# Two adapter layers on one core: when the parts of the combined weight C' are made, and which queue fetches the second weight blocks

## The reference, cut to what matters

```python
def layer0(x, ids, W0, b0, A0, B0):      # x: 8 batches x 512 tokens x 2048
    h = einsum('bsd,brd->bsr', x, A0[ids])          # rank 16
    return einsum('bsd,od->bso', x, W0) + b0 + einsum('bsr,bor->bso', h, B0[ids])

def layer1(x, ids, W1, b1, A1, B1):
    h = einsum('bti,bir->btr', x, A1[ids])
    return einsum('bti,oi->bto', x, W1) + b1 + 2.0 * einsum('btr,bro->bto', h, B1[ids])

x = x + layer0(x, itok_B_6_15, ...)
x = x + layer1(x, itok_B_0_23, ...)
```

## Time and profile before

| | |
|---|---|
| median of three executions | 2171.0 us (2167.95 to 2177.97) |
| profiled execution | 2161.93 us, span 2160.2 us, 27571 instructions |
| mean granted TensorE clock | 0.987 of full speed |
| TensorE matmul (PE) | busy 2076.9 us (96%) |
| TensorE weight load (PEld) | 1712.8 us (79%) |
| VectorE (DVE) | 1535.8 us (71%) |
| ScalarE (ACT) | 738.1 us (34%) |
| GpSimd (POOL) | 689.3 us (32%) |
| DMA | 458.03 MB, mean 212 GB/s; SyncE's queue 69.9% of 16 engines' span |

### The profile page before, as it was taken

One profiled execution on the slowest core, in us unless ns is written; L12 is line 12 of the kernel. 1 busy time (PEld: TensorE's weight loads), 2 busy tenths in 40 slices (PEclk: granted clock), 3 DMA queues, 4 the chain that ended last, 5 costly groups with the idle time before them and its releaser, 6 DMA issues.

```text
span 2160.2 us, 27571 instructions
## 1 busy us (share of the span) xinstructions
PE 2076.9 (96%) x9292; PEld 1712.8 (79%) x9292; DVE 1535.8 (71%) x2161; ACT 738.1 (34%) x1294; POOL 689.3 (32%) x498
## 2 busy tenths in 40 slices
PE   6599899999989999999999999999999999999999
PEld 5488687887878788888887888877888788888887
DVE  3367778867778876676876666875767876766875
ACT  5453232323323332333333333332333333333332
POOL 0023121544030445140544130544221445221353
PEclk9799999999999999999999999999999999999999
DMA  9974746798664699474799574789574689574676
GB/s 294 279 239 128 234 145 196 213 277 262 176 185 140 201 266 304 143 222 131 213 259 311 146 224 119 225 246 293 168 217 122 213 242 321 168 215 123 209 218 198
DMA packets 316681, 458.03 MB, mean 212 GB/s; under 512 B 27516, under 2 KB 125820, under 8 KB 316028
## 3 DMA queue, kind: packets, MB, share of 16 engines
q1 hardware_dynamic: 316284, 455.21, 69.9%
q10 hardware_dynamic: 256, 1.05, 0.3%
HBM read 381.70 MB, written 74.45 MB: 211 GB/s over the span
## 4 chain that ended last, share of the span: by engine, by line
PE 73%; DVE 9%; DMA 9%; issue 3%; SPq 2%; ACT 2%; POOL 1%; ACTq 0%; DVEq 0%; POOLq 0%
PE acc L1497 22%; PE acc L1499 21%; PE acc L1498 21%; DMA w_second<-wc_t 4%; DVE w_lo L1031 3%; DMA w_second<-v_t 2%; PE h_acc L1410 2%; PE h_acc L1414 2%; DVE c_out L1193 2%; DVE x_sum L1046 1%; DMA pb_t<-b1d_rows 1%; POOL w_raw L804 1%; DVE c_acc L1132 1%; DVE xop_lo L1056 1%; PE acc L1424 1%
## 5 line engine op out<-in xcount | busy, mean ns | idle before, releaser
L1497 PE MATMUL acc<-xop_hi,w_hi 128*128 128x512 f32 x2688 | 1055.6, 393 | 24.2 <-DVE w_lo L1031 19.1
L804 POOL TENSOR_TENSOR w_raw<-w_raw,w_second 128x512 f32<-128x512 f32 x464 | 652.3, 1407 | 1280.5 <-DMA w_second<-wc_t 862.9
L1498 PE MATMUL acc<-xop_hi,w_lo 128*128 128x512 f32 x2688 | 1048.9, 390 | 0.0
L1499 PE MATMUL acc<-xop_lo,w_hi 128*128 128x512 f32 x2688 | 1048.7, 390 | 0.0
L1031 DVE TENSOR_TENSOR w_lo<-w_raw,w_hi 128x512 fp32r<-128x512 f32 x672 | 568.3, 848 | 446.8 <-ACT w_hi L869 443.7
L869 ACT ACTIVATE w_hi<-w_raw 128x512 fp32r<-128x512 f32 x672 | 423.7, 631 | 1194.7 <-PE acc L1499 980.8
L1497 PEld LDWEIGHTS acc<-xop_hi,w_hi 128*128 128x128 f32 x2688 | 506.2, 188 | 142.1 <-DVE w_lo L1031 31.1
L1499 PEld LDWEIGHTS acc<-xop_lo,w_hi 128*128 128x128 f32 x2688 | 506.1, 188 | 106.4
L1498 PEld LDWEIGHTS acc<-xop_hi,w_lo 128*128 128x128 f32 x2688 | 506.4, 188 | 103.0
L1193 DVE TENSOR_TENSOR c_out<-acc,c_out 128x512 f32<-128x512 f32 x304 | 202.1, 682 | 7.9 <-PE acc L1424 6.2
L1046 DVE TENSOR_TENSOR x_sum<-x_in 128x512 f32<-128x512 f32 x240 | 207.5, 876 | 0.1
(11 more groups left out here) (117 smaller groups left out, 826.7 us busy)
## 6 DMA issues: line engine op xcount, KB each, us to landing
w_raw<-wc_t SPq DMA_DIRECT2D x448, 256.0 KB, 3.8
w_second<-wc_t SPq DMA_DIRECT2D x320, 256.0 KB, 5.0
w_raw<-v_t SPq DMA_DIRECT2D x208, 256.0 KB, 3.8
w_second<-v_t SPq DMA_DIRECT2D x144, 256.0 KB, 5.0
x_in<-x_t SPq DMA_DIRECT2D x128, 256.0 KB, 6.0
out_t<-c_out SPq DMA_DIRECT2D x128, 256.0 KB, 5.4
x_in<-w_t SPq DMA_DIRECT2D x64, 256.0 KB, 5.8
wc_t<-c_out SPq DMA_DIRECT2D x64, 256.0 KB, 5.5
```

The lines of the kernel that those rows point to most:

```text
L804: nc.gpsimd.tensor_tensor(w_raw[:, r, :], w_raw[:, r, :], w_second[:, n % RAW2, :], ALU.add if sign > 0 else ALU.subtract).then_inc(w_summ ...
L1497: nc.tensor.matmul(bank[:, :], wh, xh, start=(k == 0), stop=False)
L1498: nc.tensor.matmul(bank[:, :], wl, xh, start=False, stop=False)
L1499: mm = nc.tensor.matmul(bank[:, :], wh, xl, start=False, stop=end)
```

## The change

Three things are moved; no arithmetic is added or left out.

1. In passes 0 and 1 the `down` of M2 stands behind steps 5 and 7 (before 1 and 3), and the split of the following adapter in M2 in slot 12 (before 8). The four `p_add` stand 4, 9, 14 and 19 slots behind the start of M3 and M4 (before 4, 8, 12, 16), with their loads and stores.
2. The second half of `scale_c` is in M7 (before in M4). The first `turn_c` stays behind step 1 of M7, the second goes behind step 5 of M6 (before step 5 of M7), with `c_reduce` in slot 6 of M6. SyncE waits for the sums accordingly.
3. The `w_second` DMAs of all passes are issued by ScalarE's queue, in its slot g behind w_hi of step g+2, for step g+5 (before by SyncE in slot g for step g+6, behind `w_raw`). The waits are the same.

```diff
+DOWN_AT, A_SPLIT_AT = (1, 3), 8
+DOWN_LATE, A_SPLIT_LATE = (5, 7), 12
...
+        def is_late(pl, i):
+            return pl < PRE and i == M2
...
-            if j == 8 and i in DOWN and pl * 4 + DOWN_ORDER.index(i) + 1 < NPL * 4:
+            if i in DOWN and j == (A_SPLIT_LATE if is_late(pl, i) else A_SPLIT_AT) and pl * 4 + DOWN_ORDER.index(i) + 1 < NPL * 4:
...
-        P_ADD_AT = (4, 8, 12, 16)
+        P_ADD_AT = (4, 9, 14, 19)
...
+        C_TURN_AT = ((M7, 2), (M6, 6))
...
-                (oh, dh), *second = PRODUCTS[i][1]
+                oh, dh = PRODUCTS[i][1][0]
                 col = (dh * KH + h * KS) * P
                 sp.dma_start(w_raw[:, r, :], w_t[oh * MH + m, :, col:col + SW]).then_inc(wa_loaded[r], 16)
-                for oh, dh in second:
-                    n = second_no(s)
-                    if n >= RAW2:
-                        sp.wait_ge(w_summed, STEPS + n - RAW2 + 1)
-                    else:
-                        sp.wait_ge(g_turned, GROUPS)
-                    col = (dh * KH + h * KS) * P
-                    sp.dma_start(w_second[:, n % RAW2, :], w_t[oh * MH + m, :, col:col + SW]
-                                 ).then_inc(wb_loaded[n % RAW2], 16)
...
                     if pl < PRE:
-                        sp.wait_ge(c_scaled, (pl + 1) * 2 * KT)
+                        sp.wait_ge(c_scaled, (pl * 2 + (1 if i == M7 else 2)) * KT)
...
+            def load_second(s):
+
+                if not (STEPS <= s < NG and is_sum_w(s)):
+                    return
...
+                if n >= RAW2:
+                    act_e.wait_ge(w_summed, STEPS + n - RAW2 + 1)
+                else:
+                    act_e.wait_ge(g_turned, GROUPS)
+                col = (dh * KH + h * KS) * P
+                act_e.dma_start(w_second[:, n % RAW2, :], w_source(pl)[oh * MH + m, :, col:col + SW]
+                                ).then_inc(wb_loaded[n % RAW2], 16)
...
                 if g + 2 < NG:
                     w_split_hi(g + 2)
+                load_second(g + 2 + RAW2)
...
-                if pl < PRE and i in (M3, M4):
+                if pl < PRE and i in (M3, M7):
                     scale_c(pl * 2 * KT + (0 if i == M3 else KT) + j)
-                if pl < PRE and i == M7 and j in (2, 6):
-                    c_reduce(pl * 2 + (j == 6))
+                if pl < PRE and (i, j) in C_TURN_AT:
+                    c_reduce(pl * 2 + C_TURN_AT.index((i, j)))
...
-                pe.wait_ge(c_scaled, (pl * 2 + 2) * KT)
+                pe.wait_ge(c_scaled, (n + 1) * KT)
...
-                    if i in DOWN and j in (1, 3):
-                        down(q, range(0, KS) if j == 1 else range(KS, KH))
-                    if pl < PRE and i == M7 and j in (1, 5):
-                        turn_c(pl * 2 + (j == 5))
+                    down_at = DOWN_LATE if is_late(pl, i) else DOWN_AT
+                    if i in DOWN and j in down_at:
+                        down(q, range(0, KS) if j == down_at[0] else range(KS, KH))
+                    if pl < PRE and (i, j + 1) in C_TURN_AT:
+                        turn_c(pl * 2 + C_TURN_AT.index((i, j + 1)))
```

More of the change, by code:

```diff
@@ L920, in h_split_hi @@
                                      bias=h_bias[:, b:b + 1]).then_inc(h_hi_ready, 1)
+            def load_second(s):
+                if not (STEPS <= s < NG and is_sum_w(s)):
+                    return
+                q, j = divmod(s, STEPS)
+                pl, i = divmod(q, NPROD)
+                m, h = ORDER[j]
+                oh, dh = PRODUCTS[i][1][1]
+                n = second_no(s)
+                if s == M2 * STEPS:
+                    for i_v in range(2):
+                        act_e.wait_ge(v_stored[i_v], NU * 16 // 2)
+                    for i_v in range(PRAW):
+                        act_e.wait_ge(part_stored[i_v], NPART // PRAW * 16)
+                if pl == PRE and j == 0 and i in (M5, M2):
+                    for b in range(4):
+                        act_e.wait_ge(out_stored[b], (PRE if i == M2 else 1) * MH * 16)
+                if n >= RAW2:
[5 more added lines that the diff above has]
+                                ).then_inc(wb_loaded[n % RAW2], 16)
             act_e.wait_ge(ids_loaded, 32)
```

## The result

| | before | after |
|---|---|---|
| median of 13 runs (lowest to highest), us | 2168.3 (2162.5 to 2178.0) | 2156.2 (2147.9 to 2163.6) |
| ratio, 95% interval | | 0.9945 (0.9928 to 0.9962) |
| the profiled execution, us (span) | 2161.9 (2160.2) | 2159.9 (2158.2) |

The change makes the kernel faster by 12 us; 20 were forecast. Over thirteen runs the kernel before has its median at 2168.3 us, and not at the 2171.0 of the first three from which the forecast started.

A forecast was written before the change was run, and what follows sets the result against it. TensorE, busy 96%, was taken as the bound, held up by pauses in M2 and M1 of passes 0 and 1. Terms -16.5 - 8.8 + 5.4 + 0 = -19.9 us, from 2171 to 2151 us, range 2136 to 2168.

The forecast's parts named there:

- Part 1: M2 of passes 0 and 1, and a pause in M3: 19.5 us at stake, gain 16.5, ends 12 and 19.5.
- the sign: M2 and M1 of passes 0 and 1: the granted clock would be 1.00 in these stretches.
- round trip of a quarter: Store and load of a p_add quarter: 10.5 us, given 13.6 us by five slots, so VectorE's idle 5.29 and 3.81 us go.
- (d): p_add still waits or VectorE's queue stays long; half of parts 1 and 2 lost, 12.6 us: 2164 us, chance 0.09.
- What is late next: VectorE's own crowd in slots 14 and 15 of M3, falling behind by some 3 us over three slots.
- Part 2: scale_c moved from M4 to M7: gain 8.8 us at M1, loss 5.4 us in M7 over passes 0 and 1.
- price of a scale_c: One scale_c in M7 beside GpSimd's additions: 1.05 us taken, between 0.66 and 1.7, so 16.8 us for sixteen.
- the cover: VectorE in M7: 9.5 us idle plus 3.8 us of lead, 13.3 in all, absorb most of sixteen scale_c's 16.8 us.
- (a): VectorE full in M7, every scale_c meeting a GpSimd addition: 13.9 us lost in each pass, 2173 us, chance 0.10.
- Part 3: w_second issued by ScalarE in all passes: gain taken as 0, ends -8 and +15 us.
- (c): w_second's cycle was the only limit, so 9 us of M6 and M5 go: 2142 us, chance 0.19.
- (b): Transfers left on SyncE's queue come late, w_raw taking 11 us to land: 35 us lost, 2186 us, chance 0.07.

The follow-up runs named there:

- later comparison: The changed kernel, all three parts, timed once more against the kernel before: 2152.9 us against 2168.9, ratio 0.9926 (0.9903 to 0.9949).
- p1_only: Kernel before with only the later down of M2 and the quarters five slots apart: 2153.0 us against 2166.1, ratio 0.9943.
- p2_only: Kernel before with only the second half of scale_c in M7 and the second turn in M6: 2169.2 us against 2166.1, ratio 1.0014.
- scale_spread: Changed kernel with the sixteen scale_c in slots 5 to 10 of M7 and 4 to 13 of M6, second turn behind step 15: 2150.7 us.
- p3_only: Kernel before with only the w_second loads issued by ScalarE's queue: 2158.6 us against 2166.1, ratio 0.9971.
- m7_small_add: Changed kernel with GpSimd's additions for M7 of passes 0 and 1 cut to 8 of 512 columns: 2147.2 us, ratio to before 0.9894.

## Why the prediction was right, and where it wasn't

The forecast was 2151 us in a range of 2136 to 2168, and 2156.2 came out. The sum was -20 and the result -12 (-16 in the later comparison), but its three terms are off by 3 to 8 us, with both signs.

**Part 1: right in mechanism, too high** (-13.1 for -16.5 by the times; the interval reaches from 8 to 17 us). The products give less than that: M3 and M2 of both passes, where the whole term was to come from, lose 8.0 us in p1_only and 9.3 and 9.9 in the two profiles of the change. In pass 1 the change did nearly what was forecast: M2 at 51.7 and 51.1 us for 49 to 51 (51.1 to 53.9 over the nine profiles with part 1, the 53.9 in p1_only), no idle time before `down`. In pass 0 it didn't: M2 stayed at 57.4 us, with a granted clock of 0.94 where 1.00 was named as the sign. The step that failed is the round trip of a quarter, 10.5 us in 13.6. I had added up the DMAs and two issues; but in the same rows the store begins at 235.64, and the second p_add had run 3.5 us earlier. That p_add, in the kernel before and in the changed one:

```profile
232.12 0.42 DVE L1111 TENSOR_TENSOR q_half<-h_acc,q_half 128x256 f32<-128x256 f32 x1
...
235.04 0.42 DVE L1138 TENSOR_TENSOR q_half<-h_acc,q_half 128x256 f32<-128x256 f32 x1
```

The 3.1 us from its end to the issue of the store were left out; with them the time from p_add to p_add was 13.2 us already, with next to nothing to spare, and in the changed kernel it became 17.3, as the store is issued 5.2 us late there and takes 6.9 instead of 5.5 us. The rival that p_add would still wait for its quarter (d) is thus true for pass 0, and in the changed kernel for all the fourth quarters. "What is late next" was answered with VectorE's crowd; first of all it was the next quarter, and the crowd behind it.

**Part 2: gain right, cost too low.** M1's gain is 7.5 us in p2_only (97.8 to 90.3 for both passes), 6.9 and 6.0 in the two profiles of the change; 8.8 were forecast. The cost: M7 and M6 together grow by 4.9 and 4.7 us in p2_only, 9.5 us where 5.4 were forecast, by 6.8 and 18.4 in the two of the change. The price of a scale_c was right: 1.05 us taken, means of 1150 and 964 ns measured in M7 (1029 and 1017 in the second profile). What failed is the cover: "into it go 9.5 us idle and 3.8 us of lead". The lead can be spent once. The crowds at the start of M7 and of M6 spend it already, and the sixteen operations were set through all slots of M7, both boundaries included. So M7 uses up the idle time, and M6 begins with nothing in hand: its steps 1 and 2 take 5.4 and 4.1 us in pass 0, 6.2 and 4.5 in pass 1, for 2.72. scale_spread shows it from the other side: the same work at the same price between the crowds costs these two products nothing. Rival (a), VectorE full in M7, came true in what it names (48.76 busy of 49.02) at a third of its price by p2_only (9.5 of 27.8 us; two thirds and a quarter in the two profiles of the change), for not every scale_c had to meet an addition for M7 to be full.

**Part 3: the sum's zero was wrong, rival (c) right.** p3_only gives 7.5 us where (c) had 9. ScalarE's issues, changed kernel:

```profile
L945 ACTq DMA_DIRECT2D w_second<-wc_t x320: 326/326/362, 828.1 to 2137.9; - x160
...
DMA to landing us min/median/max: 2.9/4.3/7.7
```

An issue takes 0.326 us instead of the 0.43 of the earlier trace rows, and a landing 4.3 us (at most 7.7) instead of 5.0 (9.6). In the stretch where it is tight, from slot 4 of M6 to slot 1 of M5, the median of w_second went from 7.1 us before to 5.9 in p3_only and that of w_raw from 7.1 to 7.8. That is the sharing of which (b) and (c) are the two directions, and both are there: w_raw pays 0.7 us, not the 2.6 of rival (b), which has it land in 11 us for 8.5. The clean M6 of pass 3 agrees with the chain of the earlier trace rows, where one w_second took 8.7 us. That the cycle of the three w_second buffers was the limit is in the trace of the kernel before; GpSimd and the issues of w_second, late in M6 of pass 3:

```profile
1482.75 1.29 POOL L804 TENSOR_TENSOR w_raw<-w_raw,w_second 128x512 f32<-128x512 f32 x1 [2.27 <-DMA w_second<-wc_t]
...
1484.07 0.32 SPq L552 DMA_DIRECT2D w_second<-wc_t  x1
...
1487.26 1.29 POOL L804 TENSOR_TENSOR w_raw<-w_raw,w_second 128x512 f32<-128x512 f32 x1 [3.22 <-DMA w_second<-wc_t]
...
1488.57 0.32 SPq L552 DMA_DIRECT2D w_second<-wc_t  x1
```

Each load is issued 0.03 us after the addition that frees its buffer has ended, and each addition has waited for a w_second. Over the four such stretches before, 53 loads, the median from the buffer free to the issue is 0.03 us, and from the landing to the addition 0.13 us: for most of them neither SyncE's order nor its time for issuing was in the way, only the landing. In p3_only the second of these is 0.46 us, and additions wait for w_raw too. A fourth buffer wasn't tried, as there is no room for it.
The Trainium skill, "DMA: Bandwidth & Descriptors", section "Issuing engines are not separate DMA queues", says that issuing from another engine saves sequencer time and nothing else. Here the measurement differs: 0.9971 (0.9955 to 0.9988), though SyncE issued most w_second of the tight stretch as soon as the buffer was free, so it decides.

**The chances.** The prediction gave (c) 0.19 and (d) 0.09 as alternatives to the forecast. They turned out not to exclude each other: half of (d), (c), and a piece of (a) came at once, and their errors, about +3, -7 and +7 us, cancelled in part. That the time came so near is luck: only part 1's term was near, and that by the times more than by the products. The base helped as well: the forecast starts from the median of three runs, which lay 2.7 us above that of thirteen, and a gain of 20 us from 2168.3 would have been 2148.

**What stays open**: M2 of pass 0 at 55.5 us and more in every variant, where 49 is clean; how the gain of part 1 divides between its halves, and whether it gives more than what M3 and M2 lose; and why M5 of pass 1 takes over a part of what scale_spread frees.

## What to carry to other kernels

The lead of an engine over its consumer is one account for the whole boundary: before you put new work beside it, ask which crowd has drawn on it already, and place the work in the middle of a product, not over its edges (and look at the boundary behind it too). A round trip through DRAM is counted from the instruction that makes the data to the one that uses them, with the time that the store stands in its issuing queue, and the queue's other entries are looked up at the slot to which it moves. A short ring of buffers whose loads share one queue with other transfers can gain from a queue of its own even where issuing is cheap and the DMA engines are busy. The sign of it is a load that is issued the moment its buffer is free and is still the last thing waited for; try it alone, it is a small edit.

## What the runs showed of the hardware

- An operation of VectorE with two SBUF inputs (128x512, 32 bit) takes 0.69 to 0.74 us alone, and on average 0.90 to 1.15 us in M7 of the changed kernel's two profiles, where GpSimd is busy some 45% of the time with additions; those that read the accumulator (c_out) stay at 0.68 us in the same M7. Shortening GpSimd's operations is enough to get the time back (m7_small_add: 0.69 and 0.74 us until GpSimd's whole additions begin again, then up to 1.78). The Trainium skill, "SBUF — State Buffer", section "🔬 SBUF: two separate sides", describes a port that the two engines share and lock against each other; the traces agree, with 1.78 against 0.74 us at the extreme.
- Two busy queues shared the DMA engines such that the one with fewer packets gained: 7.1 to 5.9 us for it, 7.1 to 7.8 for the other (p3_only). The rate in M6 at a DMA share of 0.98 was 322 and 328 GB/s with the two queues; with one it was 316 at 0.98 and 320 at 0.99 where M6 was clean.
- The issue of a w_second took 0.43 us in the middle and up to 1.7 us on SyncE's queue, on ScalarE's 0.326 with 0.362 or 0.423 at most. A w_raw took 0.32 us on SyncE's, with the same upper end.
- The granted clock falls behind a pause: 0.94 over M2 of pass 0 (pauses of 4.4 and 1.1 us), 0.96 and 0.97 over the M6 of the first profile, 1.00 over the M1 with one pause of 1.2 us each. A part of each loss is matmuls at 1.2 instead of 2.4 GHz, which start 0.43 us apart instead of 0.23. The pause's length alone doesn't tell whether it happens: in m7_small_add it followed a pause of 2.38 us in M6 and not one of 2.33, and in scale_spread one of 1.9 us in M2 (0.97) where 2.2 us in the same place of the changed kernel had 1.00.
